# Reciprocals of the softmax row sums moved from VectorE to GpSimd, a pair of heads at a time, in a pre-norm attention and mixture-of-LoRA kernel

## What is computed

```python
scores = einsum('bhid,bhjd->bhij', q, k) * SCALE + einsum('bhid,ijd->bhij', q, rel_k)
threshold = top_k(scores, 32)[0][..., -1:]
scores = where(scores < threshold, -inf, scores)
attn = softmax(scores, axis=-1)
for i in range(3):                      # ORDER
    a_v = einsum('bhij,bhjd->bhid', attn, v_curr)
    if i == 0:
        a_v = a_v + einsum('bhij,ijd->bhid', attn, rel_v)
    v_curr = a_v
    res = res + sigmoid(alphas_raw)[i] * v_curr
```

## Time and profile before

| | |
|---|---|
| time of the profiled execution | 719.82 us |
| its span (first to last instruction) | 718.1 us |
| median of the three timed runs | 718.81 us |
| VectorE busy | 684.0 us (95%) |
| TensorE busy | 658.3 us (92%) |
| ScalarE busy | 620.5 us (86%) |
| GpSimd busy | 533.5 us (74%) |
| granted TensorE clock, mean | 0.982 |
| RECIPROCAL of line 653 | 128 times, median 157 ns |
| DMAs from issue to landing, median | diag_scratch<-a_sb 2.2 us, diag<-diag_scratch 2.2, skew<-band_scratch 2.8, band_scratch<-band 3.3 |

### The profile page before, as it was taken

The page is one execution under the profiler, slowest core; times in us unless marked ns, Lnnn a source line. Parts: engine busy times, 40 slices in busy tenths (PEclk is TensorE's granted clock), DMA queues, the critical chain, the costliest instruction groups (busy, mean ns, idle before and its releaser), DMA issues.

```text
span 718.1 us, 20880 instructions
## 1 busy us (share of the span) xinstructions
PE 658.3 (92%) x5768; PEld 513.4 (72%) x5768; DVE 684.0 (95%) x2841; ACT 620.5 (86%) x1754; POOL 533.5 (74%) x934
## 2 busy tenths in 40 slices
PE   4378999999999999999999999999999999998795
PEld 3266777777777777777777777777777777776574
DVE  6899999999999999999999999999999999999925
ACT  4588999989999899989999899989999899988833
POOL 1588898778777777877787778777878787877411
PEclk9779999999999999999999999999999999999998
DMA  6735455444544455444545454545454445454202
GB/s 204 189 106 160 128 152 154 144 149 141 151 137 148 138 147 150 136 141 144 150 134 151 133 149 137 154 130 149 137 158 140 138 134 160 129 149 116 63 13 58
DMA packets 148338, 98.72 MB, mean 137 GB/s; under 512 B 10624, under 2 KB 147968, under 8 KB 148096
## 3 DMA queue, kind: packets, MB, share of 16 engines
q1 hardware_dynamic: 147920, 97.32, 46.4%
q10 hardware_dynamic: 304, 0.08, 0.1%
HBM read 45.59 MB, written 51.77 MB: 136 GB/s over the span
## 4 chain that ended last, share of the span: by engine, by line
DVE 79%; issue 9%; PE 6%; POOL 2%; DMA 2%; ACT 1%; SPq 0%; DVEq 0%; ACTq 0%; POOLq 0%
DVE top L666 40%; DVE work L672 35%; DMA band_scratch<-zeros 1%; POOL s_sb L322 1%; DVE rinv L653 1%; PE ps_p L885 1%; PE ps_y L902 1%; PE ps_d L871 1%; PE ps_s L965 1%; ACT a_sb L435 1%; DVE stats L688 0%; PE ps_a L800 0%; DMA band_scratch<-band 0%; DMA skew<-band_scratch 0%; DVE x_sb L681 0%
## 5 line engine op out<-in xcount | busy, mean ns | idle before, releaser
L666 DVE MAX8 top<-work 128x8 f32<-128x256 f32 x768 | 285.0, 414 | 0.0
L672 DVE MATCH_REPLACE8 work<-top,work 128x256 f32<-128x256 f32 x512 | 206.1, 411 | 0.0
L322 POOL TENSOR_TENSOR s_sb<-s_sb,pen 128x512 f32<-128x512 f32 x127 | 162.1, 1276 | 55.0 <-ACT pen L425 54.6
L327 POOL TENSOR_SCALAR a_sb<-a_sb,rinv 128x256 f32<-128x256 f32 x254 | 119.6, 482 | 54.6 <-DVE rinv L653 53.7
L435 ACT ACTIVATE a_sb<-s_sb,nmax 128x256 f32<-128x256 f32 x256 | 128.1, 501 | 34.1 <-POOL s_sb L322 26.2
L425 ACT ACTIVATE pen<-s_sb,limit 128x256 f32<-128x256 f32 x254 | 116.5, 512 | 21.7 <-POOL limit L309 21.7
L297 POOL TENSOR_TENSOR s_sb<-s_sb,skew 128x384 f32<-128x384 f32 x128 | 128.6, 1004 | 3.0 <-DMA skew<-band_scratch 3.0
L885 PE MATMUL ps_p<-aT,rows 128*64 128x256 f32 x1024 | 125.1, 385 | 0.9 <-issue 0.5
L672 DVE MATCH_REPLACE8 work<-top,s_sb 128x256 f32<-128x256 f32 x256 | 103.0, 411 | 0.0
L666 DVE MAX8 top<-s_sb 128x8 f32<-128x256 f32 x256 | 94.5, 411 | 3.5 <-POOL s_sb L297 3.5
L885 PEld LDWEIGHTS ps_p<-aT,rows 128*64 128x64 f32 x1024 | 69.0, 136 | 38.5 <-issue 11.9
(11 more groups left out here) (136 smaller groups left out, 1289.9 us busy)
## 6 DMA issues: line engine op xcount, KB each, us to landing
skew<-band_scratch SPq DMA_DIRECT2D x128, 192.0 KB, 2.8
diag_scratch<-a_sb SPq DMA_DIRECT2D x128, 192.0 KB, 2.2
band_scratch<-band SPq DMA_DIRECT2D x128, 191.0 KB, 3.3
diag<-diag_scratch SPq DMA_DIRECT2D x128, 128.0 KB, 2.2
wqkv<-in_wqkv SPq DMA_DIRECT2D x1, 1152.0 KB, 7.7
x_sb<-in_x SPq DMA_DIRECT2D x4, 256.0 KB, 4.9
wout<-in_wout SPq DMA_DIRECT2D x1, 512.0 KB, 5.7
out<-xn SPq DMA_DIRECT2D x1, 512.0 KB, 3.3
```

Source lines behind the costliest of these rows:

```text
L322: nc.gpsimd.tensor_tensor(s_sb[g % 4][:], s_sb[g % 4][:], pen[g % 2][:], ALU.subtract).then_inc(pen_added, 1)
L327: nc.gpsimd.tensor_scalar(a_sb[g % 3][:, t, :], a_sb[g % 3][:, t, :], rinv[g % 2][:, t:t + 1], 1.0, ALU.mult, ALU.mult).then_inc(normed, 1)
L666: nc.vector.max(m[:, t, 8 * n:8 * n + 8], src).then_inc(top_step, 1)
L672: nc.vector.match_replace(work[t][:, n % 2, :], m[:, t, 8 * n:8 * n + 8], src, LOW).then_inc(top_step, 1)
```

## The change

Most reciprocals leave VectorE. GpSimd makes those of both heads of a pair in one TENSOR_TENSOR instruction, power with an exponent tile of -1, once both exponents are there. Both heads of pair q-1 are then normalised in slot(q) behind scale_limit(2q) and negative_max(2q+1). TensorE and ScalarE handle attention_columns(2q-2) and save_aT(2q-2) later in their slots; SyncE sends both heads together, then fetches both. scale_wout goes to the end of the slot. The last head keeps its reciprocal and its multiplies on VectorE, with semaphores of its own; the head before it gets a power of its own.

```diff
-        rsum = [sb(f"rsum{i}", [P, T]) for i in range(2)]
-        rinv = [sb(f"rinv{i}", [P, T]) for i in range(2)]
+        rsum = [sb(f"rsum{i}", [P, 2, T]) for i in range(2)]
+        rinv = [sb(f"rinv{i}", [P, 2, T]) for i in range(2)]
+        minus = sb("minus", [P, 2, T])
...
@@ SyncE slot(q)
-                if on(q - 1):
-                    send_a(2 * q - 2)
-                    fetch_diagonals(2 * q - 2)
                 if on(q + 2):
...
                 if on(q - 1):
-                    send_a(2 * q - 1)
-                    fetch_diagonals(2 * q - 1)
+                    for g in (2 * q - 2, 2 * q - 1):
+                        send_a(g)
+                    for g in (2 * q - 2, 2 * q - 1):
+                        fetch_diagonals(g)
@@ GpSimd
+            def reciprocals(p, h):
+
+                pool.wait_ge(exp_done, T * (2 * p + h))
+                reach(pool, normed, T * 2 * (p - 1))
+                nc.gpsimd.tensor_tensor(rinv[p % 2][:, 0:h, :], rsum[p % 2][:, 0:h, :], minus[:, 0:h, :],
+                                        ALU.pow).then_inc(rinv_done, 1)
...
                 if on(q):
                     add_skew(2 * q + 1)
                 if on(q - 1):
-                    normalise(2 * q - 1)
+                    reciprocals(q - 1, 2)
                 if on(q):
                     scale_limit(2 * q)
                     negative_max(2 * q + 1)
-                if 1 <= q <= NP:
-                    scale_wout(q - 1, 0, 2)
+                if on(q - 1):
+                    normalise(2 * q - 2)
+                    normalise(2 * q - 1)
                 if on(q):
                     add_penalty(2 * q)
                 if on(q + 1):
                     add_skew(2 * q + 2)
                 if 1 <= q <= NP:
-                    scale_wout(q - 1, 2, ORDER)
-                if on(q):
-                    normalise(2 * q)
+                    scale_wout(q - 1)
@@ ScalarE exponent(g) and slot(q)
-                reach(act, rinv_done, g - 1)
+                reach(act, rinv_done, g // 2 - 1)
...
                     exponent(2 * q - 1)
-                    save_aT(2 * q - 2)
...
                     save_third(q - 4)
+                if on(q - 1):
+                    save_aT(2 * q - 2)
                 if on(q - 2):
                     save_first(q - 2)
@@ VectorE top(g)
-                    if n == 2 and g > 0:
-                        divide(g - 1)
@@ TensorE slot(q)
                     scores(q + 1)
-                if on(q - 1):
-                    attention_columns(2 * q - 2)
                 if on(q - 2):
                     diagonal_columns(q - 2)
                 if on(q - 3):
                     second_power(q - 3)
                 if on(q - 4):
                     third_power(q - 4)
+                if on(q - 1):
+                    attention_columns(2 * q - 2)
                 if on(q - 2):
                     first_power(q - 2)
```

More of the change, by code:

```diff
@@ L148, in preln_attention_ffn @@
         limit_done, ramp_done, pen_added = sem("limit_done"), sem("ramp_done"), sem("pen_added")
+        last_masked, last_rinv, last_normed = sem("last_masked"), sem("last_rinv"), sem("last_normed")
         exp_done, rinv_done, normed = sem("exp_done"), sem("rinv_done"), sem("normed")
@@ L185, in preln_attention_ffn @@
         SLOTS = range(-3, PAIRS + 4)
-        MADE = 1 + 1 + 1 + 4 + 1 + 1 + 1
+        MADE = 1 + 1 + 1 + 4 + 1 + 1 + 1 + 1
         DONE = TILES - T
@@ L223, in send_a @@
             def send_a(g):
-                sp.wait_ge(normed, T * (g + 1))
+                if g < HEADS - 1:
+                    sp.wait_ge(normed, T * (g + 1))
+                else:
+                    sp.wait_ge(last_normed, T)
                 if g < DRING:
@@ L290, in _ @@
             nc.gpsimd.memset(warm[:], 1.0).then_inc(made, 1)
+            nc.gpsimd.memset(minus[:], -1.0).then_inc(made, 1)
+            pool.wait_ge(made, MADE)
             def add_skew(g):
@@ L322, in add_penalty @@
                 nc.gpsimd.tensor_tensor(s_sb[g % 4][:], s_sb[g % 4][:], pen[g % 2][:], ALU.subtract).then_inc(pen_added, 1)
+            def reciprocals(p, h):
[3 more added lines that the diff above has]
+                                        ALU.pow).then_inc(rinv_done, 1)
             def normalise(g):
-                pool.wait_ge(rinv_done, g + 1)
+                p = g // 2
+                pool.wait_ge(rinv_done, p + 1)
                 for t in range(T):
-                    nc.gpsimd.tensor_scalar(a_sb[g % 3][:, t, :], a_sb[g % 3][:, t, :], rinv[g % 2][:, t:t + 1], 1.0,
+                    nc.gpsimd.tensor_scalar(a_sb[g % 3][:, t, :], a_sb[g % 3][:, t, :], rinv[p % 2][:, g % 2, t:t + 1], 1.0,
                                             ALU.mult, ALU.mult).then_inc(normed, 1)
@@ L336, in clip_block, with scale_wout @@
                 nc.gpsimd.tensor_tensor(clip[p % 2][:], src, mask[:], ALU.mult).then_inc(clipped, 1)
-            def scale_wout(hp, a, e):
+            def scale_wout(hp):
                 pool.wait_ge(alpha_done, 1)
                 pool.wait_ge(wout_in, 16 * 2)
-                for i in range(a, e):
+                for i in range(ORDER):
                     nc.gpsimd.tensor_scalar(wk[:, i, hp, :], wout[:, hp, :], al[:, hp, i:i + 1], 1.0, ALU.mult,
@@ L391, in _ @@
             add_skew(2 * q + 1)
-            normalise(2 * q - 1)
+            reciprocals(q - 1, 2)
             scale_limit(2 * q)
             negative_max(2 * q + 1)
+            normalise(2 * q - 2)
+            normalise(2 * q - 1)
             add_penalty(2 * q)
+            reciprocals(q, 1)
             normalise(2 * q)
@@ L428, in exponent @@
             def exponent(g):
-                act.wait_ge(pen_added, g + 1)
+                if g < HEADS - 1:
+                    act.wait_ge(pen_added, g + 1)
+                else:
+                    act.wait_ge(last_masked, 1)
                 act.wait_ge(nmax_done, g + 1)
@@ L432, in exponent @@
                 ring(act, diag_out, g - 3)
-                reach(act, rinv_done, g - 1)
+                reach(act, rinv_done, g // 2 - 1)
                 for t in range(T):
                     nc.scalar.activation(a_sb[g % 3][:, t, :], s_sb[g % 4][:, t, :], ACT.Exp, bias=nmax[g % 2][:, t:t + 1],
-                                         scale=1.0, accum_out=rsum[g % 2][:, t:t + 1]).then_inc(exp_done, 1)
+                                         scale=1.0, accum_out=rsum[g // 2 % 2][:, g % 2, t:t + 1]).then_inc(exp_done, 1)
             def save_queries(p):
@@ L648, in _, with divide_last @@
             STEPS = T * (2 * ROUNDS - 1)
-            def divide(g):
+            def divide_last(g):
                 dve.wait_ge(exp_done, T * (g + 1))
-                reach(dve, normed, T * (g - 1))
-                nc.vector.reciprocal(rinv[g % 2][:], rsum[g % 2][:]).then_inc(rinv_done, 1)
+                nc.vector.reciprocal(rinv[g // 2 % 2][:, g % 2, :], rsum[g // 2 % 2][:, g % 2, :]).then_inc(last_rinv, 1)
             def top(g):
@@ L699, in mask_last @@
                                                 PENALTY, ALU.is_lt, ALU.mult))
-                nc.vector.tensor_tensor(s_sb[g % 4][:], s_sb[g % 4][:], pen[g % 2][:], ALU.subtract).then_inc(pen_added, 1)
+                nc.vector.tensor_tensor(s_sb[g % 4][:], s_sb[g % 4][:], pen[g % 2][:], ALU.subtract).then_inc(last_masked, 1)
             def normalise_last(g):
-                dve.wait_ge(rinv_done, g + 1)
+                dve.wait_ge(last_rinv, 1)
                 for t in range(T):
-                    nc.vector.tensor_scalar(a_sb[g % 3][:, t, :], a_sb[g % 3][:, t, :], rinv[g % 2][:, t:t + 1], None,
-                                            ALU.mult).then_inc(normed, 1)
+                    nc.vector.tensor_scalar(a_sb[g % 3][:, t, :], a_sb[g % 3][:, t, :],
+                                            rinv[g // 2 % 2][:, g % 2, t:t + 1], None,
+                                            ALU.mult).then_inc(last_normed, 1)
             def second_normal(a, e):
@@ L763, in _ @@
             second_normal(0, 4)
-            divide(HEADS - 1)
+            divide_last(HEADS - 1)
             normalise_last(HEADS - 1)
@@ L795, in attention_columns @@
             def attention_columns(g):
-                pe.wait_ge(normed, T * (g + 1))
+                if g < HEADS - 1:
+                    pe.wait_ge(normed, T * (g + 1))
+                else:
+                    pe.wait_ge(last_normed, T)
                 reach(pe, t_saved, g)
```

## The result

| | before | after |
|---|---|---|
| median of the runs | 718.87 us | 809.3 us (809.07 to 811.05) |
| ratio, with its 95% interval | | 1.127 (1.125 to 1.128), slower |
| span of the profiled execution | 718.1 | 807.4 |
| VectorE, TensorE, ScalarE, GpSimd busy | 684.0, 658.3, 620.5, 533.5 | 687.4, 666.5, 626.4, 590.5 |

The changed kernel is 90 us slower. The forecast was slower, 781 us, range 766 to 820. Every engine did about as much work as before, but for GpSimd, which did 57 us more; on VectorE and TensorE the 89 us by which the span grew are waits. From the page after, the costliest groups: out<-in, count | busy us, mean ns | idle us before them, and what ended it.

What follows compares the result with a forecast made beforehand. VectorE and TensorE bound the kernel, nearly full, with GpSimd leading by under 1 us. A loop of 11.2 us a pair added 61.7 and the tail 0.6 to 719.8: 782.1, less 1.0 to the median, 781; range 766 to 820.

Steps and rivals of the forecast that it cites:

- the loop: Late multiplies delay transposes, powers_back, save_rows, ramp, add_penalty, add_skew and the next odd head: 11.2 us a pair, not 10.08; chance 0.65.
- the sum: Heads 5 to 127: 61 pairs at 11.2 us, 683.2, plus 3.6 for project's extra matmuls, 686.8 against 625.1 now.
- The reciprocal's 0.07 a head: RECIPROCAL holds VectorE's stream 0.07 us; removing 127 saves 8.9 us if VectorE stayed the bound, 4.97 a head.
- The power: GpSimd's 128x4 power, taken as 0.4 us between 0.19 and 1.28, with about 0.7 of cover, so free at 0.4.
- rival A: A slow power on GpSimd: beyond 0.7 us it pushes negative_max and the loop; 817 at 1.28 us; chance 0.18.
- The even half: GpSimd from negative_max through four multiplies, add_penalty and add_skew: 5.10 plus 0.04 handover, alone a 10.1 us pair, no change.
- TensorE's stretch: TensorE from head 2q-2's transposes, through first_power, to the end of powers_back: 4.99 us, ending at E + 7.00, E the odd head's start.
- The rest at nothing: ScalarE's later copies, SyncE's sends and fetches, scale_wout and the memset stay beside the loop or under cover, costing nothing.
- B: TensorE's later slot is absorbed, the even half rules at 10.1 us a pair, time about 720; chance 0.04.
- C: TensorE's wait absorbed and GpSimd passes the even half by E + 4.93: VectorE bound at 4.97 a head, 711; chance 0.05.
- D: TensorE's clock falls from idling some 1.4 us a pair: its 4.99 becomes 8.5, about 995 us; chance 0.03.
- E: GpSimd stands still once at its first power to load code: 4 to 8 us, about 788; chance 0.05.

Runs made afterwards that it cites:

- e12: The kernel with GpSimd powers per head, limits ahead of multiplies and ramp ahead of the score copies, its 24 output-weight scalings moved two to a slot: 716.7 us, ratio 0.9979.
- e1: The changed kernel with the power replaced by a multiply of the same two 128x4 tiles: 792.8 us, ratio 1.102.
- e6: The kernel before with only the moves of TensorE, ScalarE and SyncE, GpSimd and VectorE untouched: 727.5 us, ratio 1.013.
- the probe: The kernel before with extra GpSimd powers of 1 to 64 columns and one multiply in its idle start, into a spare tile: 727.6 us.

## Why the prediction was right, point by point

Right in direction, in the loop and in its links; 28 us low in size. The loop's own error had been put at 12 us. What was missing is more than twice that and all on one side, so that 809 stands in the part of the range that had been kept for a slow power, and the slow power brought 15 us of the 27. Between the starts of heads 5 and 127 the trace after has 710.7 us (46.49 to 757.24), where the sum said 686.8.

- **What bounds the kernel**: two engines without cover, and GpSimd's lead of 0.96 and 0.71 us over VectorE. Right: both waits of VectorE in the changed kernel (1.15 and 0.25 a pair) end with an add_skew that came later than its lead.
- **The reciprocal's 0.07 a head**: right, and no gain. A head without it took 4.97 where nothing stalled it (e12).
- **The power**: taken at 0.4, within the bounds of 0.2 and 1.28, measured 1.01. Its cover, put at 0.7, was nearly right: only 0.24 showed in the pair (negative_max at E + 1.07), 0.23 by the multiply, so the cover was 0.77. This is the term that was mis-sized, 61 x 0.24 = 15 us. It is rival A, at 0.24 a pair where A had 0.6 for a power of 1.28.
- **The even half**: forecast 5.14 without an excess of the power; measured 5.10 with the multiply, 5.32 (302.15 to 307.47) with the power.
- **TensorE's stretch** from the transposes to the end of powers_back: forecast 4.99, measured 5.13 (304.38 to 309.51). The transposes take 0.59 of stream in front of first_power, not 0.49, and first_power 1.67, not 1.62: two stream times that I took from other neighbours. 61 x 0.12, net of the rest of the loop, is 7 us; e1 shows it alone, 11.32 against 11.2.
- **The end of the loop**: the sum gave the last pair 11.2 like the others. It took 14.55 (742.69 to 757.24), 3.0 more than the pairs in the middle, and the rows show two causes of about 1.5 each. TensorE's stretch took 6.75 (745.21 to 751.96) instead of 5.13, with a granted clock of 0.66 over most of it. Then ScalarE loaded the table of its square root, 1.28 us ahead of the ramp that the loop waits for, and a second one ahead of the next exponent. In the kernel before the same two loads stood there too and held VectorE for 0.89 in front of the RECIPROCAL at 670.20. Head 127 so waited 3.88 instead of 1.15, and TensorE then 4.53, behind which it ran at the slow clock:

```profile
745.00:750.00 5.00, 4.79 (x32) 3.74 (x33) 4.48 (x18) 2.45 (x9) 3.41 (x6) 0.66 0.45 135
```

```profile
752.60 1.28 ACT L554 ACT_TABLE_LOAD   x1
```

```profile
757.24 0.75 DVE L685 MAX8 top<-s_sb 128x8 f32<-128x256 f32 x2 [3.88 <-POOL s_sb L303]
```

```profile
759.76 1.05 PE L821 MATMUL ps_a<-ident,a_sb 128*128 128x128 f32 x4 [4.53 <-POOL a_sb L341]
760.74 1.98 PE L892 MATMUL ps_d<-aT,v_sb 128*64 128x256 f32 x8
```

  That is 2.7 us ahead of head 127, and a tail of 50.2 us for 47.2, forecast 47.8: another 2.4. With 15, 7 and 0.6 at the start these add to 28, for the 27 us by which the span was longer than the forecast. The shares of the clock and of the table loads are read from the rows, not tried.
- **The rest at nothing**: wrong for the moves of TensorE, ScalarE and SyncE, which alone cost 9 us (e6). Inside the changed kernel this cost doesn't show: the second transposes start without a wait there (306.64), since ScalarE, which was waiting, copies the first at once (305.07; in e6 at 306.79).
- **Rivals B and C** (absorbed, faster): nothing of either; TensorE's wait was 1.57 a pair for the 1.4 forecast. **D**, the clock: not in the middle (1.00), but in slot 62 (0.66 from 745 to 750), and all along the run one power further (0.90 on the mean). **E**: refuted by the first power of the probe.

## What to carry to other kernels

An engine with idle time isn't an engine with room: GpSimd was idle a quarter of the time before, and yet one head's multiplies, made 6.5 us later with TensorE's transposes still in front of powers_back, cost 75 us, since each of its calls frees another engine and the leads were under 1 us. With the transposes moved out of the way the same order of GpSimd cost nothing, and gained nothing. Follow a moved step through every queue it enters until it meets its own wait again: a loop that closes within one pair is paid in every pair. And where a wait must sit somewhere, release others first (the limit ahead of the multiplies, the ramp ahead of the copies): that order was worth some 44 us here (762.0 to 717.5), with the same instructions.

## What the runs showed of the hardware that was not expected

- A power on GpSimd costs 0.158 us a column of 128, on 0.41 fixed, where an add costs 0.0021 a column (0.27 for 128 columns): 75 times as much. Its price lies in the columns, and 64 of them take 10.5 us.
- TensorE's clock under a repeated wait: waits of 1.57 us a pair left it at 1.00, of 2.7 us brought 0.91 on the mean, with either level behind waits of the same length, and of 4.04 us 0.84. An engine made to wait a little longer thus lost as much again by its clock: 1.1 us of added work a pair cost 2.2.
